# Keys projected in the first three steps of a pair, values of all four row tiles in the fourth

## The reference

```python
ln_out = _ln(hidden_states, ln_w, ln_b)
q = _ln(_fp8_linear_pertensor(ln_out, wq, wq_scale, q_in_scale).reshape(b, s, g, hpg, d))
k = _ln(_fp8_linear_pertensor(ln_out, wk, wk_scale, k_in_scale).reshape(b, s, g, d))
v = _fp8_linear_pertensor(ln_out, wv, wv_scale, v_in_scale).reshape(b, s, g, d)
core = _gqa(q, k, v).reshape(b, s, nh * d)
```

## Time and profile before

| | |
|---|---|
| time, median of 3 runs | 1814.33 us (1813.86 to 1814.97) |
| time of the profiled execution | 1810.02 us |
| its span | 1807.7 us |
| mean granted TensorE clock | 0.998 |
| first step of block 2 begins | 338.9 us |
| pair 14 (group 3, third sequence) | 908.2 to 946.6 us |

### The profile page before, as it was taken

One profiled execution on the slowest core, in us unless ns is written; L12 is line 12 of the kernel. 1 busy time (PEld: TensorE's weight loads), 2 busy tenths in 40 slices (PEclk: granted clock), 3 DMA queues, 4 the chain that ended last, 5 costly groups with the idle time before them and its releaser, 6 DMA issues.

```text
span 1807.7 us, 32021 instructions
## 1 busy us (share of the span) xinstructions
PE 1746.5 (97%) x10933; PEld 1238.5 (69%) x11048; DVE 1410.3 (78%) x4581; ACT 1126.1 (62%) x2570; POOL 271.6 (15%) x429
## 2 busy tenths in 40 slices
PE   9999999888999999999999999999999999989997
PEld 4444445666887787777777787787778778755554
DVE  1243526689889887888888888888888888879996
ACT  1141415476777776677777667767767766557776
POOL 0000000211111111111111111111111112101111
PEclk9999999999999999999999999999999999999999
DMA  7000000111212120121112112111210112000000
GB/s 268 24 1 24 0 1 25 36 36 37 84 59 81 62 96 5 51 73 36 32 42 73 38 36 73 36 43 30 75 41 19 61 54 84 13 1 19 24 24 30
DMA packets 45599, 83.35 MB, mean 46 GB/s; under 512 B 3584, under 2 KB 22528, under 8 KB 45056
## 3 DMA queue, kind: packets, MB, share of 16 engines
q1 hardware_dynamic: 45440, 81.31, 13.7%
HBM read 69.77 MB, written 10.49 MB: 44 GB/s over the span
## 4 chain that ended last, share of the span: by engine, by line
PE 72%; DVE 11%; issue 9%; ACT 5%; POOL 2%; DMA 0%; POOLq 0%; ACTq 0%
PE bank L536 16%; PE bank L592 10%; PE bank L634 8%; PE bank L680 5%; PE bank L612 4%; PE bank L716 3%; PE bank L410 3%; PE bank L496 3%; PE bank L470 3%; PE bank L458 3%; PE bank L488 3%; PE bank L598 3%; PE bank L571 3%; PE bank L437 2%; PE bank L565 1%
## 5 line engine op out<-in xcount | busy, mean ns | idle before, releaser
L978 ACT ACTIVATE pr<-bank,nmx 128x512 f32<-128x512 f32 x256 | 174.6, 690 | 137.1 <-DVE nmx L1354 135.8
L536 PE MATMUL bank<-wqs,XQ 128*128 128x256 f16 x2048 | 245.1, 273 | 4.7 <-DVE x L1239 4.7
L592 PE MATMUL bank<-prT,KV 128*128 128x256 f32 x1024 | 243.4, 381 | 0.0
L634 PE MATMUL bank<-kT,qT 128*128 128x512 f32 x512 | 240.9, 593 | 0.9 <-issue 0.9
L536 PEld LDWEIGHTS bank<-wqs,XQ 128*128 128x128 bf16 x2048 | 197.0, 98 | 43.3 <-DVE x L1239 11.8
L592 PEld LDWEIGHTS bank<-prT,KV 128*128 128x128 f32 x1024 | 190.3, 191 | 50.4 <-issue 22.0
L1524 POOL TENSOR_TENSOR rdev<-gvar,cst 128x7 f32<-128x7 f32 x128 | 191.2, 1493 | 10.0
L1522 POOL TENSOR_TENSOR gvar<-mvB,geps 128x7 f32<-128x7 f32 x128 | 29.2, 228 | 1075.3 <-DVE mvB L1199 1068.3
L966 ACT ACTIVATE yb<-bank,rsT 128x128 bf16<-128x128 f32 x512 | 147.0, 378 | 57.0 <-PE bank L598 57.0
L1354 DVE TENSOR_REDUCE nmx<-bank 128x1 f32<-128x512 f32 x256 | 166.5, 680 | 6.2 <-PE bank L634 3.8
L680 PE MATMUL bank<-identf,pr 128*128 128x128 f32 x1024 | 151.5, 276 | 18.8 <-DVE pr L1219 18.2
(11 more groups left out here) (179 smaller groups left out, 3202.1 us busy)
## 6 DMA issues: line engine op xcount, KB each, us to landing
wa<-in_wgu SPq DMA_DIRECT2D x32, 512.0 KB, 3.7
wst<-in_wcat SPq DMA_DIRECT2D x21, 512.0 KB, 4.1
wpst<-in_wproj SPq DMA_DIRECT2D x8, 1024.0 KB, 6.4
wa<-in_wdn SPq DMA_DIRECT2D x16, 512.0 KB, 3.7
xT<-in_xT SPq DMA_DIRECT2D x4, 1024.0 KB, 6.9
wkx<-in_wkvx SPq DMA_DIRECT2D x8, 512.0 KB, 4.9
tern_gu<-wa SPq DMA_DIRECT2D x16, 256.0 KB, 2.0
wgu<-tern_gu SPq DMA_DIRECT2D x2, 2048.0 KB, 7.3
```

What stands on the lines that cost most here:

```text
L536: ins = mm(dst, XQ[:, b, c, k, j * P:(j + 1) * P], w, start=(k == 0 and m == 0), stop=(k == KT - 1 and m == 1))
L592: mm(OB[:, 0:2 * P], KV[:, n % 2, t, P:2 * P], prT[:, st % 2, t, :, :].rearrange("p h s -> p (h s)"), start=(t == 0), stop=(t == ST - 1))
L634: mm(SB_[h][:], qT[:, h, st * P:(st + 1) * P], kT[:, :], start=True, stop=True).then_inc(s["scores_made"], 1)
L978: act_f(pr[:, h, :], SB_[h][:], ACT.Exp, bias=nmx[:, st, h:h + 1], accum_out=su[:, st, h:h + 1]).then_inc(s["exp_done"], 1)
```

## The change

Keys and values are no longer projected together by row tile. Steps 0, 1 and 2 of a pair project the keys alone, of the same row tiles as before (8, 16 and 8 matmuls of 128 columns), and step 3, which projected neither, projects the values of all four row tiles (32 matmuls into the four quarters of `P1`). The number of matmuls is the same.

With it go: `kv_copy` has four parts instead of three, the fourth copies 512 columns of values, the others copy 128, 256 and 128 columns of keys; the counts of `kv_out` and `proj_kv_made` go up by four per pair; the halves of the weight part with keys and values are cut by keys and values instead of by contraction tiles (four splits of 128 columns in each half as before), and the keys' projection waits for the first half only; the values' projection waits for `kxt_out`, since `P1` also holds the transposed cross keys.

```diff
-KVPART = ((0,), (1, 2), (3,), ())
+KPART = ((0,), (1, 2), (3,), ())
...
+        def half_of(part, half):
+            if part % 3 == 2:
+                return [((K, V)[half], k) for k in range(KT)]
+            return [(WPART[part % 3][0], 2 * half), (WPART[part % 3][0], 2 * half + 1)]
...
             def proj_kv(n, part):
-                if 3 * n + part:
-                    pe.wait_ge(s["kv_out"], 3 * n + part)
-                if n % NB == 0 and part == 0:
-                    pe.wait_ge(s["wl_ready"], 6 * (n // NB) + 6)
+                if n or part:
+                    pe.wait_ge(s["kv_out"], 4 * n + part)
+                if n % NB == 0 and part in (0, 3):
+                    pe.wait_ge(s["wl_ready"], 6 * (n // NB) + (5 if part == 0 else 6))
...
-                for i, j in enumerate(KVPART[part]):
-                    for c, lo in ((K, 0), (V, P)):
-                        ins = project(P1[:, 256 * i + lo:256 * i + lo + P], c, n, j)
+                if part == 3:
+                    if n:
+                        pe.wait_ge(s["kxt_out"], n // 2 + 1)
+                    for t in range(ST):
+                        ins = project(P1[:, t * P:(t + 1) * P], V, n, t)
+                else:
+                    for i, t in enumerate(KPART[part]):
+                        ins = project(P1[:, i * P:(i + 1) * P], K, n, t)
                 ins.then_inc(s["proj_kv_made"], 1)
...
                     def next_proj():
                         if T >= 3:
                             pe.wait_ge(s["acc_done"], T - 2)
-                        if st < 3:
-                            proj_kv(n + 1, st)
+                        proj_kv(n + 1, st)
                         pe.wait_ge(s["raw_out"], 4 * n + 4 + st)
                         proj_q(n + 1, st)
...
             def kv_copy(n, part, par):
-                if KVPART[part]:
-                    act.wait_ge(s["proj_kv_made"], 3 * n + part + 1)
-                    lo, hi = KVPART[part][0], KVPART[part][-1] + 1
-                    copy(KV[:, par, lo:hi, :].rearrange("p t c -> p (t c)"), P1[:, 0:256 * (hi - lo)]).then_inc(s["kv_out"], 1)
+                act.wait_ge(s["proj_kv_made"], 4 * n + part + 1)
+                if part == 3:
+                    copy(KV[:, par, :, P:2 * P], P1[:, :].rearrange("p (t c) -> p t c", t=ST)).then_inc(s["kv_out"], 1)
+                else:
+                    lo, hi = KPART[part][0], KPART[part][-1] + 1
+                    copy(KV[:, par, lo:hi, 0:P], P1[:, 0:P * (hi - lo)].rearrange("p (t c) -> p t c", c=P)).then_inc(s["kv_out"], 1)
```

More of the change, by code:

```diff
@@ L349, in fetch_tern @@
                 sp.wait_ge(s["proj_q_made"], 4 * (TT - 3 + i))
-                sp.wait_ge(s["proj_kv_made"], 3 * (TT - 3 + i))
+                sp.wait_ge(s["proj_kv_made"], 4 * (TT - 3 + i))
                 if i < 2:
@@ L519, in stage_a @@
                         pe.wait_ge(s["raw_out"], j)
-                    if j < 3:
-                        proj_kv(0, j)
+                    proj_kv(0, j)
                     proj_q(0, j)
@@ L582, in turn_kx @@
                 pe.wait_ge(s["nq_ready"], 4 * n + 1)
-                pe.wait_ge(s["kv_out"], 3 * n + 3)
+                pe.wait_ge(s["kv_out"], 4 * n + (3 if n else 4))
                 nc.tensor.transpose(P1[:, 256:256 + P], kxn[:, :], identf[:]).then_inc(s["kxt_made"], 1)
@@ L705, in pair @@
                             if b % 2:
-                                pe.wait_ge(s["kv_out"], 3 * n + 3)
+                                pe.wait_ge(s["kv_out"], 4 * n + 4)
                                 if b == 3:
@@ L799, in copy, with split_high @@
                 return act_f(dst, src, ACT.Copy)
-            def split_high(part, ks):
+            def split_high(part, half):
                 act.wait_ge(*part_loaded(part))
-                for c in WPART[part % 3]:
-                    for k in ks:
-                        ins = act_f(split_weights(part // 3, c, k)[0], staged(part, c, k), ACT.Copy, scale=srel[:, c, k:k + 1])
+                for c, k in half_of(part, half):
+                    ins = act_f(split_weights(part // 3, c, k)[0], staged(part, c, k), ACT.Copy, scale=srel[:, c, k:k + 1])
                 ins.then_inc(s["wh_ready"], 1)
@@ L911, in _ @@
             for part in range(3):
-                split_high(part, (0, 1))
-                split_high(part, (2, 3))
+                split_high(part, 0)
+                split_high(part, 1)
                 if part < 2:
@@ L1031, in pair @@
                     if b < 3 and not last and st in (2, 3):
-                        split_high(3 * (g + 1) + b, (0, 1) if st == 2 else (2, 3))
+                        split_high(3 * (g + 1) + b, st - 2)
                     if st == 0:
@@ L1174, in split_low @@
                 dve.wait_ge(s["wh_ready"], 2 * part + half + 1)
[L1175 to L1179, removed]
+                for c, k in half_of(part, half):
+                    wh, wl = split_weights(part // 3, c, k)
+                    ins = v.scalar_tensor_tensor(out=wl, in0=staged(part, c, k), scalar=srel[:, c, k:k + 1],
+                                                 in1=wh, op0=ALU.mult, op1=ALU.subtract)
                 ins.then_inc(s["wl_ready"], 1)
@@ L1186, in head_stats @@
                 slots = list(range(4))
-                for i, t in enumerate(KVPART[j]):
+                for i, t in enumerate(KPART[j]):
                     if i == 0:
-                        dve.wait_ge(s["kv_out"], 3 * n + j + 1)
+                        dve.wait_ge(s["kv_out"], 4 * n + j + 1)
                     v.bn_stats(bnB[:, 4 + i, :], KV[:, par, t, 0:P])
```

## The result

The changed kernel takes 1844.95 us (median of 4, 1843.61 to 1846.36) against 1814.57 us before (4 runs): ratio 1.0168, 95% interval 1.015 to 1.0186. The forecast was 1850, range 1838 to 1862. The profiled executions are 36.15 us apart (1846.17 and 1810.02), the medians 30.4.

The account below looks back on a forecast made before the run. Bound: a VectorE chain from `px` to step 3's `accumulate` nearly even with TensorE, then TensorE alone. 7.12 - 2.25 - 0.3 = 4.6 us per four pairs, 36 us over 31 pairs, plus 1810.02 and 4.3: 1850 us, range 1838 to 1862.

Parts of the forecast that it names:

- Gain 0 in step 0: Step 0: removing 8 matmuls (0.45 us) gains 0; even pairs wait for the query copy, odd pairs' VectorE chain starts unmoved.
- Steps 1 and 2 bring only the distance to the `accumulate`: TensorE gets ahead, then waits at step 3's `accumulate`; only 2.25 us is recovered in pairs 12 to 15 together.
- The small remainders: Short VectorE waits for TensorE, at step 3's `accumulate` and in even pairs' step 1 rounding, go: 0.3 us less per four pairs.
- The chain: VectorE's fixed-order work from scaling `px` in step 1 to the `accumulate` opening step 3: 18.3 us, nearly even with TensorE.
- The block in step 3 counts in full: Step 3: the 32 added matmuls behind the wait for `acc_done` cost their full 1.78 us per pair, 7.12 per four pairs.
- The sum by the weight loads' share: A rule weighed: weight loads fill 6.30 of 8.20 us in step 3, so 2 us could hide the values; sum 0 or less.
- ScalarE's copy, the halves: 0: Step 3's 0.59 us values copy is covered by ScalarE's idle 1.26 us, and the recut split halves cost nothing: 0.
- The sum: Whole kernel: 4.6 us per four pairs, 1.14 per pair, 35.4 over 31 pairs; with exceptions of +0.6, 36 us.
- The offset: Whole kernel: the median of the runs before stood 4.3 us above the profiled execution, so 1846.0 became 1850 us.
- Rival D: New TensorE idle stretches in each pair halve the clock: 1.5 us per pair, 46 us more, 1896 us; chance 0.03.

## Why the prediction was right

*Gain 0 in step 0.* Held: even pairs wait for the query copy instead, and step 0 of pair 14 keeps its length. In odd pairs step 0 does get shorter (pair 13: 12.43 to 11.98 us), and the wait at the turn of the probabilities takes it back, as forecast.

*Steps 1 and 2 bring only the distance to the `accumulate`.* Held, and it is the step on which the sign rests. Four pairs: predicted 7.12 - 2.25 - 0.3 = 4.57 us, measured 4.49. The small remainders, an estimate of 0.3, measure 0.48: the stretch from `px` to the `accumulate` is shorter by 0.25, 0.01, 0.16 and 0.06 us in pairs 12 to 15. The chain is shown from both sides: shortened, the changed kernel gains 16 us; lengthened, the kernel before loses 25 us. Of the 5.2 us that the second adds per four pairs 2.8 are lost; the rest went into TensorE's distances.

*The block in step 3 counts in full.* Held: 1.57 us for 28 matmuls. One sign given for it was wrong, though: step 3 was to be longer by about 1.3 to 1.8 us, and it is longer by 2.1 to 2.5. The block's 1.78 us and the new wait of 0.35 to 0.68 us both stand in it; 1.3 would have been the pair's cost and not the step's. The sum by the weight loads' share (a quarter of the step free) is refuted for this stretch.

*ScalarE's copy, the halves: 0.* Held, the halves by their run, the copy by the 1.09 us that ScalarE has to spare behind it.

*The sum.* 31 pairs at 1.14 was a little high. In pairs 2 to 7 no extra VectorE instruction stands ahead of the `accumulate`, the distance was 0.76 us in all but pair 4, and they cost 0.84 to 0.98. Pairs 2 to 28 together: 28.7 us against 27 x 1.14 = 30.8 (pair 4, forecast at about half of 1.14, cost 0.91). Pairs 29 and 30: 3.4, as predicted. That all 31 pairs still sum to 35.7 in the traces, beside the 36 forecast, is in part luck: pair 0 contains 2.8 us of a lower clock (below), and pair 1, forecast at 1.7, shows -0.1, because the kernel before had the additional stretch at half the clock there.

*The offset.* What I added to get from the profiled execution to the median, 4.3 us, was not a property of the kernel. Later runs of the kernel before went from 1809.3 to 1816.1 us. The difference of the profiled executions was the 36 that I forecast; the difference of the medians 30.4. The mean granted clock was 0.998 in the profiled execution before and 0.996 in the one after; from that, 0.002 x 1830 = 3.7 of the 36 us are clock (an estimate). The 32.5 that are left are nearer to the medians. So the forecast of 1850 was 5 us too high, mostly by the offset of 4.3.

*Rival D.* Not as a rule: no clock fall in the steady pairs. But pair 0 is 3.7 us longer after the change: 2.85 us in step 0, where the clock was at half, and 0.89 in step 3, where the values stand and the clock was not.

## What to carry to other kernels

Where two engines are nearly even over a stretch, what counts in moving work is on which side of their meeting point it lies: taken from the fuller engine beside the other's chain it brings only the distance at the next wait between them, behind that wait it costs its full length. Where the next wait is for something that the move doesn't bring forward, as for the query copy in step 0 of pair 14, it brings nothing. Read that distance (end of the releasing instruction to the start of the released one) before moving anything; it gave 4.57 us for four pairs where the trace then showed 4.49. And fill waits from the stretch behind them, ahead of the chain's start, which is what gave 0.55% here.

## What I had not expected

The clock differs from execution to execution, and mostly at the same few places. Busy time by window at the first step of block 2, the kernel before (first fence) and the changed kernel (second): a granted clock of 1.00 against 0.50, that is 2.4 against 1.2 GHz, for the first score matmuls; a second stretch at 0.50 follows at 346.8.

```profile
340.00:343.30 3.30, 0.90 (x4) 0.07 (x2) 3.04 (x9) 1.56 (x4) 2.95 (x6) 1.00 0.58 206
```

```profile
340.00:343.30 3.30, 3.30 (x4) 0.89 (x4) 1.04 (x5) 0.68 (x2) 2.48 (x7) 0.50 0.88 323
346.80:350.10 3.30, 3.30 (x22) 3.23 (x20) 0.00 (x0) 1.82 (x4) 0.00 (x0) 0.50 0.00 0
```

Timeline, the same matmuls, before and after. TensorE had been idle for as long ahead of them in both, until ScalarE's key copy was done, and took 1.96 us for them in one and 3.65 in the other; why the clock differed stays open:

```profile
338.92 1.96 PE L634 MATMUL bank<-kT,qT 128*128 128x512 f32 x4 [0.92 <-issue]
```

```profile
339.82 3.65 PE L643 MATMUL bank<-kT,qT 128*128 128x512 f32 x4 [0.91 <-issue]
```

Step 0 of pair 0 costs 2.85 us more with it. The kernel with the halves alone, whose pairs from 12 to 28 agree with the kernel before to 0.01 us, was at half the clock there for longer and loses 3.7 us in the same step. The changed kernel without the clamps was not, and its step 0 of pair 0 takes 10.20 us, 10.19 in the kernel before. So these few us come and go without the change. The spread of the whole times goes with the clock too: in 17 executions of the kernel before, the three with a mean granted clock of 0.998 took 1809.3 to 1809.7 us and the one with 0.994 took 1816.1; 0.004 of 1810 us would be 7.2 (an estimate). A comparison by pairs without such a stretch is sharper than one by the whole time.
